# Mean layers issued row tile by row tile in a fixed order, with the degree work and all one-hot stores in the first block of a four-block graph network

## Time and profile before

| | us |
|---|---|
| median of 3 runs | 1022.16 (1020.14 to 1029.8) |
| the profiled execution | 1020.54 |
| its span, first to last instruction | 1018.8 |
| TensorE busy | 849.1 (83%) |
| VectorE busy | 702.8 (69%) |
| ScalarE busy | 516.1 (51%) |
| mean granted clock of TensorE | 0.898 |

### The profile page before, as it was taken

One profiled execution on the slowest core, in us unless ns is written; L12 is line 12 of the kernel. 1 busy time (PEld: TensorE's weight loads), 2 busy tenths in 40 slices (PEclk: granted clock), 3 DMA queues, 4 the chain that ended last, 5 costly groups with the idle time before them and its releaser, 6 DMA issues.

```text
span 1018.8 us, 13452 instructions
## 1 busy us (share of the span) xinstructions
PE 849.1 (83%) x3591; PEld 617.1 (61%) x3591; DVE 702.8 (69%) x1257; ACT 516.1 (51%) x990; POOL 332.0 (33%) x286
## 2 busy tenths in 40 slices
PE   2979788788888597891699999999999999999692
PEld 2666255556766485670466766658656766668572
DVE  7997656669645564448688768986698768875405
ACT  2376104436354332324677557765677557753622
POOL 3000645665013022133635026520754046512100
PEclk9989659779778799796799999999999999999797
DMA  5412457576125031242668128860778138741001
GB/s 113 135 30 92 117 165 231 162 228 187 35 73 189 0 97 68 64 147 66 140 162 199 51 73 228 181 186 4 213 187 202 63 112 206 182 117 42 1 1 51
DMA packets 59303, 122.24 MB, mean 120 GB/s; under 512 B 9104, under 2 KB 22706, under 8 KB 59237
## 3 DMA queue, kind: packets, MB, share of 16 engines
q0 software_dynamic: 20048, 52.18, 21.9%
q1 hardware_dynamic: 36165, 63.88, 20.7%
q10 hardware_dynamic: 3024, 5.31, 1.4%
HBM read 105.61 MB, written 15.74 MB: 119 GB/s over the span
## 4 chain that ended last, share of the span: by engine, by line
PE 70%; DVE 17%; ACT 7%; issue 4%; DMA 1%; another core or an unknown queue 0%; SPq 0%; DVEq 0%; ACTq 0%
PE ps L1009 15%; PE ps L692 13%; PE ps L986 10%; PE ps L1025 6%; PE ps L1041 6%; PE ps L845 5%; PE ps L816 4%; PE ps L942 2%; PE ps L797 2%; PE ps L684 2%; DVE st L1604 2%; DVE z_parts L1760 2%; ACT slot_recs L1103 2%; PE ps L786 1%; PE ps L861 1%
## 5 line engine op out<-in xcount | busy, mean ns | idle before, releaser
L1009 PE MATMUL ps<-z_parts,onehot_dst 128*125 128x512 f32 x664 | 204.5, 413 | 5.7 <-issue 2.0
L692 PE MATMUL ps<-w,xT 128*125 128x512 f32 x660 | 173.8, 422 | 8.2 <-DVE w L1358 4.9
L1760 DVE SCALAR_TENSOR_TENSOR z_parts<-ps,z_parts 128x512 fp32r<-128x512 f32 x216 | 147.8, 688 | 39.9 <-ACT z_parts L1257 32.0
L986 PE MATMUL ps<-x_parts,gather_lhs 128*128 x432 | 140.1, 409 | 40.6 <-DVE x_parts L1739 31.5
L1257 ACT ACTIVATE z_parts<-ps 128x512 fp32r<-128x512 f32 x216 | 128.3, 597 | 76.0 <-PE ps L986 59.5
L692 PEld LDWEIGHTS ps<-w,xT 128*125 128x125 f32 x660 | 130.3, 201 | 42.0 <-issue 10.4
L1009 PEld LDWEIGHTS ps<-z_parts,onehot_dst 128*125 128x125 f32 x664 | 110.1, 185 | 72.0 <-issue 53.7
L643 POOL DMA_INDIRECT gathered<-rel_rows,rowi x83 | 89.4, 1078 | 151.6 <-DMA rel_rows<-x_cur 96.5
L658 POOL DMA_INDIRECT queued<-node_rows,srci x60 | 95.7, 1594 | 88.2 <-ACT queued L1180 72.7
L986 PEld LDWEIGHTS ps<-x_parts,gather_lhs 128*128 128x128 f32 x432 | 78.8, 189 | 73.4 <-issue 57.4
L621 POOL TENSOR_TENSOR w<-w_stage,w 128x512 fp32r<-128x512 f32 x36 | 48.1, 1368 | 199.5 <-ACT w L1058 199.5
(11 more groups left out here) (275 smaller groups left out, 1245.2 us busy)
## 6 DMA issues: line engine op xcount, KB each, us to landing
w_stage<-in_weights SPq DMA_DIRECT2D x88, 256.0 KB
onehot_dst<-onehot_rows SPq DMA_DIRECT2D x80, 250.0 KB
onehot_rows<-onehot_dst ACTq DMA_DIRECT2D x20, 250.0 KB
gather_lhs<-edge_src_rows SPq DMA_DIRECT2D x8, 432.0 KB, 8.0
node_rows<-work SPq DMA_DIRECT2D x20, 160.0 KB, 2.0
queued<-node_rows,srci POOLq DMA_INDIRECT x116
node_rows<-work SPq DMA_DIRECT2D x20, 90.0 KB, 2.0
rel_rows<-rel_rows_out SPq DMA_DIRECT2D x10, 160.0 KB, 1.9
```

What stands on the lines that cost most here:

```text
L692: mm = pe.matmul(ps[0:R, bank, :], lt[:, a, k, n * R:(n + 1) * R], w[:, b, k, :], start=first and k == 0 and (a, b) == THREE[0], stop=last ...
L986: mm = pe.matmul(ps[:, 5 + t % 3, :], L[:, t, :], XS[:, a, bass.ds(s, 1), :], start=a == HI, stop=a == LO)
L1009: mm = pe.matmul(ps[0:R, d, :], S[:, j // SK % SR, j % SK, :], Z[:, g % ZR, a, :], start=False, stop=False, skip_group_check=True)
L1760: v.scalar_tensor_tensor(out=Z[:, g % ZR, LO, :], in0=of, scalar=0.0, in1=Z[:, g % ZR, HI, :].bitcast(F32), op0=ALU.max, op1=ALU.subtract) ...
```

## The change

Six edits, made together.

1. Edge loop. The gather ring grows from 20 to 23 buffers (three lie in x_cur's place); a gather of the first round waits for counting group `i // 3` in place of `2 * (i - 1) // 5`. The fills stand at every fourth tile (`FILL_AT = 4 * j`, the last at tile 56). All 21 groups of one-hots are stored from the loop; `onehots_again` goes. Weights 7 are split in the loop (from tile 62).
2. Degree work in the loop. The 3125-wide maximum comes at tile 6, the parts of adjT at tiles 8 to 31, and from tile 62 on `deg_rows` sums adjT with 20 matmuls of some 313 columns into 34 equal rows, from which the degree columns come by five small transposes; the low-block steps follow at tiles 67 to 76. The 50 one-column matmuls, `DG4`, the round trip of the degree rows through HBM and their waits go.
3. Mean layers. TensorE: x_tile 0 of the next layer stands before mean_tile 4, x_tile 1 behind it, then y 0, x 2, y 1, x 3, y 2, x 4, y 3, y 4. VectorE and ScalarE follow one written order (`normed_rows`, `mean_rows`) in which a row tile's `head`, `finish`, `low` and `y` steps stand between those of others.
4. The layer norm in block 1: VectorE does `(ps - mean) * gain` in one pass and `* rstd + shift` in a second one; ScalarE's pass L1072 of these layers and one VectorE pass per tile go.
5. Weights: VectorE makes the low parts of 7 to 12 (`w_lows`), between the layers; matrix 13 is loaded behind `node_rows(0)` and split inside the loop of block 2, as in its other layers. The row of We has its own place and is loaded behind block 0. GpSimd keeps 20 and 21.
6. After the last mean layer, head, second norm and parts of x run tile by tile (`part_low(n - 2)` inside the loop). Block 3 uses `normed_rows` as well; ScalarE's `w_highs(21)` now stands behind all `y_high` of the block.

```
-GR = 20
+GR = 23
-MADE = (0, 5, 9, 15, NG)
-FILL_AT = [0] + [j * (TE - 4) // (NREL * NT - 1) for j in range(1, NREL * NT)]
+MAX_AT, HIGH_AT, DEG_AT = 6, (8, 13, 18, 23, 28), 62
+W4_AT, W5_AT, W6_AT, W7_AT = 4, 22, 44, 62
+FILL_AT = [4 * j for j in range(NREL * NT)]
...
-                    gp.wait_ge(c_used, min(2 * (i - 1) // 5, NCF + NCL - 1))
+                    gp.wait_ge(c_used, min(i // 3, NCF + NCL - 1))
...
-            for j in range(7, 12):
-                w_lows(j)
...
+            def deg_rows():
+                pe.wait_ge(at_made, NT)
+                pe.wait_ge(self_out, NREL * NT)
+                for h, bank in ((0, 7), (1, 5)):
+                    for s in range(NT):
+                        for a in (HI, LO):
+                            mm = pe.matmul(ps[0:DP, bank, 0:314 - 2 * h], one34[0:R, :],
+                                           AT[0:R, a, s, 313 * h:314 + 311 * h],
+                                           start=s == 0 and a == HI, stop=s == NT - 1 and a == LO)
+                mm.then_inc(deg_done, 1)
...
             def mean_layer(l, follow):
                 y_tile(l, 0)
+                x_tile(l, 2)
+                y_tile(l, 1)
                 x_tile(l, 3)
-                y_tile(l, 1)
+                y_tile(l, 2)
                 x_tile(l, 4)
-                y_tile(l, 2)
                 y_tile(l, 3)
                 y_tile(l, 4)
...
                 for n in range(NT):
+                    if follow and n == NT - 1:
+                        x_tile(l + 1, 0)
                     mean_tile(l, n)
-                    if follow and n >= 2:
-                        x_tile(l + 1, n - 2)
+                if follow:
+                    x_tile(l + 1, 1)
...
-                if t % SK == SK - 1 and t // SK < MADE[1]:
+                if t % SK == SK - 1 or t == TE - 1:
                     s_store(t // SK)
+                if t in HIGH_AT:
...
+            def normed_rows(l, roots, ready, xs):
+                root(0, roots + 1)
+                for n in range(NT):
+                    normal(X[0:R, n, :], H[0:R, n, :], n, ready + n + 1, x_made)
+                    by_degree(n, xs + n + 1)
+                    if n < NT - 1:
+                        root(n + 1, roots + n + 2)
+                    tr_high(n, XT, n, TR_MEAN[l] + n + 1)
+                    if n >= 2:
+                        y_high(5 + (n - 2) % 3, n - 2, Y_L1[l] + n - 1)
...
+            normed_rows(NL1, NT * (NL1 + 2), 2 * NT, XM_L3)
             w_highs(21)
-            mean_parts(NL1)
...
+            def head(l, n):
+                v.wait_ge(o_done, NT * l + n + 1)
+                stats(ps[0:R, n, :], n)
+                v.wait_ge(ln_var, v_stats(l, n))
+                v.scalar_tensor_tensor(out=H[0:R, n, :], in0=ps[0:R, n, :], scalar=mv[0:R, n, 0:1], in1=ROW[0:R, 0, :],
+                                       op0=ALU.subtract, op1=ALU.mult)
...
+            def affine(l, n):
+                v.wait_ge(ln_sd, v_stats(l, n))
+                link(v.reciprocal(rstd[0:R, n:n + 1], sd[0:R, n:n + 1]))
+                link(v.scalar_tensor_tensor(out=H[0:R, n, :], in0=H[0:R, n, :], scalar=rstd[0:R, n:n + 1],
+                                            in1=ROW[0:R, 1, :], op0=ALU.mult, op1=ALU.add))
...
-                    if l and i in W2_LOW:
+                    if i in W2_LOW:
                         w_low(13 + 2 * l, W2_LOW.index(i))
```

More of the change, by code:

```diff
@@ L857, in _ @@
                 mm.then_inc(agg_done, 1)
-            pe.wait_ge(self_out, NREL * NT)
-            for n in range(NT):
-                for s in range(NT):
-                    mm = pe.matmul(ps[0:R, 7, n:n + 1], TC[0:R, s, n * R:(n + 1) * R], onef[0:R, 0:1],
-                                   start=s == 0, stop=s == NT - 1)
-            mm.then_inc(deg_done, 1)
             def x_tile(l, n):
@@ L1044, in _ @@
                             mm.then_inc(w2_done, 1)
-            for n in range(3):
+            for n in range(2):
                 x_tile(NL1, n)
@@ new lines, in mean_rows, with top, rows, high @@
+            def mean_rows(l):
+                def top(n):
+                    root(n, NT * l + n + 1, epsd)
+                def rows(n):
+                    by_degree(n, XM_L1[l] + n + 1)
+                def high(n):
+                    tr_high(n, XT, n, TR_MEAN[l] + n + 1)
+                def y(n):
+                    y_high(5 + n % 3, n, Y_L1[l] + n + 1)
+                top(0)
+                rows(0)
+                top(1)
+                rows(1)
+                top(2)
+                high(0)
+                high(1)
+                rows(2)
+                top(3)
+                y(0)
+                high(2)
+                rows(3)
+                y(1)
+                high(3)
+                top(4)
+                y(2)
+                rows(4)
+                high(4)
+                y(3)
+                y(4)
@@ new lines, in low, with y, normed_rows @@
+            def low(l, n):
+                tr_low(n, XT, n, TR_MEAN[l] + n + 1)
+            def y(l, n):
+                y_low(5 + n % 3, n, Y_L1[l] + n + 1)
+            def normed_rows(l, roots, start, end):
+                start(0)
+                end(0)
+                start(1)
+                scale(0, roots + 1)
+                end(1)
+                start(2)
+                scale(1, roots + 2)
+                low(l, 0)
+                end(2)
+                start(3)
+                scale(2, roots + 3)
+                low(l, 1)
+                end(3)
+                start(4)
+                scale(3, roots + 4)
+                low(l, 2)
+                end(4)
+                y(l, 0)
+                scale(4, roots + 5)
+                low(l, 3)
+                y(l, 1)
+                low(l, 4)
+                for n in range(2, NT):
+                    y(l, n)
@@ new lines, in between @@
+            def between(l):
+                w_lows(8 + 2 * l)
+                if l:
+                    v.wait_ge(l_raw, 16 * LCH)
+                    for c in range(LCH // 2 * (l - 1), LCH // 2 * l):
+                        set_lhs(c)
+                if l < NL1 - 1:
+                    w_lows(9 + 2 * l)
+                v.wait_ge(row_in, 32 * (l + 1))
+            for l in range(NL1 - 1):
+                between(l)
+                v.wait_ge(b_made, NT)
+                head(l, 0)
+                finish(l, 0)
+                head(l, 1)
+                finish(l, 1)
+                head(l, 2)
+                low(l + 1, 0)
+                finish(l, 2)
+                low(l + 1, 1)
+                head(l, 3)
+                finish(l, 3)
+                low(l + 1, 2)
+                y(l + 1, 0)
+                head(l, 4)
+                low(l + 1, 3)
+                finish(l, 4)
+                y(l + 1, 1)
+                low(l + 1, 4)
+                for n in range(2, NT):
+                    y(l + 1, n)
@@ L1738, in _, with part_low @@
+            l = NL1 - 1
+            between(l)
+            def part_low(n):
                 v.wait_ge(xs_hi, n + 1)
@@ L1740, in _ @@
                                 ALU.subtract).then_inc(xs_made, 1)
+            for n in range(NT):
+                head(l, n)
+                if n:
+                    scale(NT + n - 1, NT * NL1 + SECOND[n - 1])
+                affine(l, n)
+                v.wait_ge(sum_made, n + 1)
+                link(v.scalar_tensor_tensor(out=H[0:R, n, :], in0=H[0:R, n, :], scalar=0.0, in1=B[0:R, n, :],
+                                            op0=ALU.max, op1=ALU.add))
+                stats(H[0:R, n, :], NT + n)
+                if n >= 2:
+                    part_low(n - 2)
+            scale(2 * NT - 1, NT * NL1 + SECOND[NT - 1])
+            part_low(NT - 2)
+            part_low(NT - 1)
             def queue_add(l, k):
@@ L1808, in _ @@
                     w_lows(14 + 2 * l)
-                for n in range(NT):
-                    if l < NL2 - 1:
+                if l < NL2 - 1:
+                    for n in range(NT):
                         v.wait_ge(xs_hi, NT * (l + 1) + n + 1)
```

424 lines of the change are left out of this document (165 added, 259 removed).

## The result

The changed kernel took 994.3 us (median of four runs, 988.0 to 1002.2) where the kernel before, run beside it, took 1023.1: a ratio of 0.971, with a 95% interval of 0.963 to 0.980. The forecast was 967.4 with a range of 950 to 988, so the gain is real, but it is little more than half of what was predicted, and the time lies outside the range. The profiled execution took 994.3, its span is 992.5.

A forecast was written before the change was run, and what follows sets the result against it. The prediction took the kernel as bound by TensorE, except where TensorE waits, and priced those waits: 1020.5 + 6 - 22 - 30.6 - 12.5 + 1 + 5 = 967.4 us, with a range of 950 to 988.

The forecast's parts named there:

- Part 1: Edge loop: added work, early fills and VectorE's maximum make it 6 us longer, between 8 shorter and 16 longer.
- my 30 us: Edge loop behind tile 57: VectorE's lows, one-hots, weights and degree work together 30 us, against some 29 before.
- C: Edge loop: the added stores slow the gathers, 22 us in place of the 6, total 983; chance 12%.
- B: Edge loop not longer: early fills sit in stalls, ring of 23 helps, -8 in place of +6, total 953; 15%.
- A: Row-tile passes: fixed orders tie three engines into longer chains, one more 1.2 us round per tile, 18 us, total 985; 12%.
- D: Edge loop: each store triggers a late ring release, 16 x 5.3 = 85 us, slower than before at 1052; 2%.
- Part 2: Edge loop to layer 0: degree matmuls go, y 0 starts 8.1 us behind the loop, 42.2 us against 64.2; -22 us.
- Part 3: Mean layers 0 to 1 and 1 to 2: 45.7 us each against 61.0, by_degree waits gone; 30.6 us less together.
- Part 4: Last mean layer to block 2: 30.6 us in place of 43.2, VectorE working tile by tile; -12.5 us.
- Block 2, +1 predicted: Block 2's first loop takes weights 13 along, which adds 1 us.
- Part 5: Block 3: y 0 starts earlier, but z waits 6.7 us for GpSimd's low parts of matrix 21; +5 us.
- I take these stalls as staying: Edge loop: ScalarE's cast waits for TensorE's late ring releases, 40.9 us, up to 5.3 at once, were assumed to remain.

The follow-up runs named there:

- c2_late_max: Changed kernel with the 3.4 us maximum at tile 34 in place of 6 and adjT's high parts at tiles 38 to 54: 954.6 us, ratio 0.956.
- e2: The kernel of c2_late_max again, nothing else, on the chip with late releases: 977.1 us, ratio 0.952 to the kernel before.
- b1_stores: Kernel before, with the 16 later groups of one-hots stored in the edge loop and not made again in the mean layers: 1002.4 us, ratio 1.002.
- d2_late_again: c2_late_max with only five groups of one-hots stored in the loop, 16 made and stored again in the mean layers: 973.0 us, ratio 0.946.
- e3: e2 with ScalarE splitting matrix 21 between block 3's tiles in place of behind the last y high part: 963.3 us, ratio 0.939.
- the controls: The changed kernel with nothing edited, run again on two chips: 971.3 us (ratio 0.973) and 992.8 us (ratio 0.967).
- b2_fills: Kernel before, with self products every four tiles and weights 5 and 6 split at tiles 22 and 44: 1000.9 us, ratio 1.003.
- first and second groups: Eight edited or control kernels on two chips without late releases, beside the kernel before at 999.5 and 998.5 us; 954.6 to 1002.4 us.
- third and fourth groups: Eight edited or control kernels on one chip with late releases, beside the kernel before at 1027.5 and 1024.9 us; 963.3 to 1027.5 us.

## Why the prediction was wrong, point by point

**Part 1, edge loop: +6 predicted, +31 measured. This is the step that failed.** Its sentence was "GpSimd issues a gather every 1.25 us or so (1.03 plus the issue gap) and is 22 tiles ahead". That took the issue's duration from the earlier trace rows as fixed, while the part itself put a 3.4 us maximum and five low parts into VectorE's early tiles. The duration was up to 5.3 us beside the backlog, and the lead, my cover for the whole loop, was gone. Two terms can be told apart. The long issues: 114.3 less 98.2, so 16 us, without late releases; 137.9 less 117.4, so 20.5, with them (17 to 25, given the scatter), and there most of it as late releases that I had taken as staying. The added work: c2_late_max's 98.2 less 87 of the old order, so 11 us, and e2's 117.4 less 106.8 of the kernel before, so 11 again; I had taken 6 between bounds of -8 and 16. Half of it or more lies behind tile 57 (5.8 of e2's 10.6). There my 30 us came true (e2 30.7, c2 30.2), but the "some 29 that these tiles took before" was misread: the trace of the kernel before has 24.9. Up to tile 57 e2 takes 86.8 us, the kernel before 82.0. The bounds held for the work; no bound held the issues, because I looked for a price of the stores and of TensorE's releases, and never asked what GpSimd needs while VectorE is full.

**Rivals.** C had a size near the measured one (22 in place of 6, 983), but the wrong mechanism: b1_stores moves every store at once and loses nothing. By the Trainium skill ("DMA: Bandwidth & Descriptors", section on queues, rings and completion order) each DMA engine takes turns between its queues, which was the rule behind C; no run here shows that it cost anything: in b1_stores 279 GB/s went through beside TensorE at full clock, and d2_late_again, with 16 stores fewer in the loop, has a ratio of 0.946 for 0.952, with intervals that overlap. B's hope for idle time to fill failed too. A did not come: the orders held, with one wait of 1.39 us a layer where 1.5 was worked out. D did not come as priced: no store cost 3.3 us. Late releases did grow, to waits of 10.6 us where 5.3 was the most, but with the long issues and not with the stores.

**Start of the program, not priced:** the counting ended 1.4 us earlier.

**Part 2: -22 predicted, -20.5 measured.** y 0 started 10.95 us behind the bias matmuls, not 8.1; the products between were 1.3 us shorter (30.9 for 32.1):

```profile
303.64 1.09 PE L670 MATMUL ps<-ident,work 125*128 125x125 f32 x4 [2.13 <-ACT work L1068]
304.39 4.26 PE L678 MATMUL ps<-w,xT 128*125 128x512 f32 x12
...
315.56 19.75 PE L678 MATMUL ps<-w,xT 128*125 128x512 f32 x84
```

The step left out TensorE's wait for the second tile's transposes, 2.13 us, which now stand before y 0.

**Part 3: -30.6 predicted, -31.8 measured** (two times 45.2 for 61.0 and 61.3). All by_degree waits of 3 us are gone. **Part 4: -12.5 predicted, -12.4 measured.** Both were right in mechanism and size.

**Block 2, +1 predicted, +6.6 measured.** From its first matmul to the end of its last product 457.1 us, before 450.5. In the 13 other traces with the changed order of block 2 it took 452.1 to 460.7, in the three others with the old order 454.0 to 456.1. So most of the 6.6 is scatter: the profile of before lies under every other trace, of either order. The means of the two kinds differ by 2.5 us (456.3 and 453.7), which this scatter doesn't clear.

**Part 5: +5 predicted, +2.9 measured.** The wait is there as described, 6.30 us:

```profile
945.34 15.77 PE L678 MATMUL ps<-w,xT 128*125 128x512 f32 x60 [6.30 <-POOL w L610]
```

The half clock behind it cost 1.4 us (15.77 for 14.4), not 2.5. e3 shows that the order gains once the wait is taken away.

**The base.** The sum was made on an execution of a chip with late releases, and I took them as the kernel's. That did no harm to the ratio: 0.971 there, 0.973 and 0.967 for the controls. But a fifth of the loop (20 of 107 us) was the chip's own, and "I take these stalls as staying" hid that TensorE has little slack without them.

## What to carry to other kernels

When work is moved to VectorE beside gathers that GpSimd issues, ask not only whether VectorE has the time, but whether it will run a backlog of instructions with two SBUF operands; the gather's issue time may then be no constant, and the lead in buffers is what pays for it. Keep long single instructions out of the first tiles, where a backlog then meets dense work (moving one from tile 6 to tile 34, with the low parts behind it, was worth 17 us), or break the run with instructions that read nothing from SBUF; 60 ns each were enough here. And run the kernel before on the same chip as each experiment: an absolute time from another chip was off by some 25 us.

## What the runs showed of the hardware

- A gather issue on GpSimd takes 0.95 us, and took 2.7 to 5.3 us beside some gapless runs of two-operand VectorE instructions (seven in a row in the first profile), not beside others (23.0 us in b1, 35.8 in c2). Six of the seven ended 0.15 to 0.17 us behind the next instruction with a large operand from PSUM. With 81 writes of one column, 59 ns each, put in, no issue took over 1.5 us, and GpSimd's busy time in the loop fell from 85.3 to 56.0 us.
- TensorE's releases came late in the profiles of some chips and not of others. In the 8 traces of the first and second groups' chips all 83 releases of the loop are recorded and the old order's loop takes 87 us; in the 8 traces of the third and fourth groups, one chip, 66 to 74 are recorded, and 70 and 77 in the two first profiles, whose loops take 107 and 138 us. The runs of the kernel before, 998 to 1000 there and 1023 to 1028 here, go with it. The largest delays (18 to 30 us) stand in the three traces of them where GpSimd issued for 47 us or more without a pause. That pauses would end them was not tried, and why they come stays open.
- A share of 0.85 of the DMA engines' time, at 279 GB/s (b1_stores), took nothing from a loop whose gathers come through the same engines: 86.9 us, against 87.5 at 0.74 and 231 GB/s (b2_fills).
